# Moving the rotary exchange to SBUF-to-SBUF DMAs, and its addition, a gate polynomial and two splits to GpSimd and ScalarE, in a software-pipelined attention and expert block

## The reference

```
q, k, v = silu(causal_conv4(x @ Wq)), silu(causal_conv4(x @ Wk)), silu(causal_conv4(x @ Wv))
q, k = rope(q, cos, sin), rope(k, cos, sin)      # pairs (x1, x2) -> (x1 c - x2 s, x1 s + x2 c)
q, k = q / |q|, k / |k|
beta  = sigmoid(x @ bw + bb)
alpha = exp(-exp(A_log) * softplus(x @ gkw + gkb + dt_bias))
S     = alpha * (S - beta * k (k S)) + beta * k v      # per token, o = q S + D (q.k) v
y     = ((x @ Wg) * silu(o * rsqrt(mean(o*o)) * onorm_w)) @ Wo
```

## Time and profile before

| what | value |
|---|---|
| profiled execution, time | 5533.59 us |
| its span, first to last instruction | 5531.7 us |
| median of three runs | 5533.1 us |
| mean granted TensorE clock | 0.843 of 2.4 GHz |
| TensorE, VectorE busy | 87%, 84% of the span |
| ScalarE, GpSimd busy | 62%, 38% of the span |
| mean DMA | 36 GB/s |

### The profile page before, as it was taken

How to read it: one execution, slowest core, us unless ns; L and a number is a source line. 1 busy time by engine, 2 the same in 40 slices (tenths; PEclk the granted TensorE clock), 3 DMA queues, 4 the chain that set the end, 5 groups by cost and what they waited for, 6 DMA issues and landing times.

```text
span 5531.7 us, 111231 instructions
## 1 busy us (share of the span) xinstructions
PE 4792.2 (87%) x40448; PEld 3609.5 (65%) x40448; DVE 4623.1 (84%) x11457; ACT 3445.0 (62%) x6166; POOL 2085.5 (38%) x1485
## 2 busy tenths in 40 slices
PE   4688889988889898889898899888899888899986
PEld 2466667666667666667666677666677666677665
DVE  6888898888888888988888988888988888988852
ACT  3456666656666656766666666566666666666653
POOL 3443333443343442343443344433434433334420
PEclk7778898888888888988888888878988888888878
DMA  1001111011111011111111111111111011111011
GB/s 59 10 11 34 43 43 34 28 32 37 43 43 34 24 32 41 43 33 32 33 33 42 43 33 32 32 34 43 43 34 32 32 34 43 43 34 32 31 34 56
DMA packets 214453, 197.13 MB, mean 36 GB/s; under 512 B 13848, under 2 KB 176416, under 8 KB 209696
## 3 DMA queue, kind: packets, MB, share of 16 engines
q1 hardware_dynamic: 213920, 190.01, 11.1%
HBM read 148.02 MB, written 4.19 MB: 28 GB/s over the span
## 4 chain that ended last, share of the span: by engine, by line
DVE 52%; PE 38%; issue 8%; ACT 1%; SPq 0%; DMA 0%; POOL 0%; DVEq 0%; POOLq 0%; ACTq 0%
PE bank L984 36%; DVE acc L1390 10%; DVE tmpb L1556 6%; DVE NP L1526 6%; DVE Gam L1559 5%; DVE mx L1653 3%; DVE Gam L1512 3%; DVE moe L1738 2%; PE bank L988 2%; DVE QK L1671 1%; DVE QK L1479 1%; DVE Gam L1563 1%; DVE rot L1475 1%; DVE ms L1603 1%; DVE Kt L1543 1%
## 5 line engine op out<-in xcount | busy, mean ns | idle before, releaser
L1390 DVE SCALAR_TENSOR_TENSOR acc<-bank,conv_w,acc 128x255 f32<-128x255 f32 (+2 forms) x2304 | 925.1, 470 | 27.3 <-ACT acc L791 26.4
L717 POOL TENSOR_TENSOR sq<-acc 128x256 f32<-128x256 f32 x256 | 191.2, 747 | 1734.5 <-ACT acc L797 1722.3
L984 PE MATMUL bank<-QK 64*128 64x256 f32 (+1 forms) x4096 | 603.3, 352 | 211.8 <-DVE mx L1653 97.7
L984 PE MATMUL bank<-W,h 128*128 128x128 f32 x4096 | 579.7, 302 | 190.1 <-issue 103.3
L984 PEld LDWEIGHTS bank<-W,h 128*128 128x128 f32 x4096 | 551.7, 215 | 237.1 <-issue 129.6
L984 PE MATMUL bank<-mT,W 128*128 128x256 f32 x2048 | 626.4, 447 | 60.3 <-issue 39.7
L984 PEld LDWEIGHTS bank<-QK 64*128 64x128 f32 (+1 forms) x4096 | 288.6, 142 | 523.7 <-issue 346.0
L966 ACT ACTIVATE h<-bank,b 128x256 f32<-128x256 f32 x1024 | 416.7, 479 | 288.6 <-PE bank L984 286.7
L984 PEld LDWEIGHTS bank<-mT,W 128*128 128x128 f32 x2048 | 420.9, 220 | 219.2 <-issue 155.3
L729 POOL TENSOR_TENSOR rot<-rot,sin 128x512 f32<-128x512 f32 x256 | 337.3, 1317 | 450.8 <-DVE rot L1475 450.8
L1559 DVE TENSOR_TENSOR Gam<-Gam,tmpb 128x31 f32<-128x31 f32 (+15 forms) x992 | 448.1, 452 | 34.1
(11 more groups left out here) (226 smaller groups left out, 10275.4 us busy)
## 6 DMA issues: line engine op xcount, KB each, us to landing
W<-in_W SPq DMA_DIRECT2D x512, 256.0 KB, 3.2
QK<-QK SPq DMA_DIRECT2D x32, 1024.0 KB, 5.1
xin<-in_x SPq DMA_DIRECT2D x32, 128.0 KB, 4.7
x<-in_x SPq DMA_DIRECT2D x32, 128.0 KB, 2.1
xnG<-xnT SPq DMA_DIRECT2D x32, 128.0 KB, 1.9
out<-moe SPq DMA_DIRECT2D x32, 128.0 KB, 1.9
NP<-in_c_alpha_sel SPq DMA_DIRECT2D x1, 1024.0 KB, 5.4
Wqkv<-in_Wq SPq DMA_DIRECT2D x1, 512.0 KB, 6.1
```

Source lines behind the costliest of these rows:

```text
L984: return mm(out_, lhsT, rhs, start=first, stop=last)
L1390: v.scalar_tensor_tensor(acc[:, n % 2, m, j:T], ps[:, m, 0:T - j], conv_w[:, kind, c, PAD - j:KT - j], acc[:, n % 2, m, j:T], ALU.mult, AL ...
```

## The change

It has five parts and a new set of tables.

1. **Exchange**: `swap` leaves VectorE. SP issues two DMAs for each chunk, `acc` odd partitions to `rot` even ones and the reverse.
2. **Addition**: `rope` leaves VectorE for GpSimd, behind the sin product.
[...]
4. **Splits**: `maxes` goes to GpSimd (6 operations). Of `fqk` the two casts go to ScalarE (`part`), the last difference to GpSimd (`part2`), one difference stays. Of `alphaT` four copies go to ScalarE (`al`), three operations stay.
5. **Constants**: the scale 1/64 of the mean square goes into ScalarE's Square, so two small VectorE operations (L1609) go; the factor 2 goes into `neg_A`.

`ORDER` and `BANK` are replaced as a whole; they still span 35 turns. The load of `xnG` waits for four `g` and four `v` products of the sequence before instead of one `g`.

```diff
 ORDER = {
     "sp": """
-        xnG:0@1 x1:0@3 expert:1@3 expert:0@3 expert:2@3 expert:3@3 expert:4@3 expert:5@3 QK1:0@1 store:0@3 expert:7@3
-        expert:6@3 xin:0@0""",
+        swap:5@1 swap:6@1 xnG:0@1 expert:1@3 x1:0@3 swap:7@1 expert:0@3 expert:2@3 expert:3@3 swap:0@0 expert:4@3
+        QK1:0@1 swap:1@0 expert:5@3 swap:2@0 expert:6@3 store:0@3 swap:3@0 expert:7@3 xin:0@0 swap:4@0""",
...
@@ sync
+            def swapped(k, n):
+                sp.wait_ge(a_silu.sem, a_silu.at(k, n + 1))
+                if begun(k, n - 1):
+                    sp.wait_ge(p_QK.sem, p_QK.at(k, n - 1))
+                for q in range(2):
+                    sp.dma_start(rot[q::2, n % 2], acc[1 - q::2, n % 2]).then_inc(rot_in[n % 2][q].sem, 16)
@@ gpsimd
             def by_sin(k, c):
-                pool.wait_ge(v_rot.sem, v_rot.at(k, c + 1))
+                for q in range(2):
+                    pool.wait_ge(rot_in[c % 2][q].sem, rot_in[c % 2][q].at(k, 16 * (c // 2 + 1)))
...
+            def turned(k, c):
+                pool.wait_ge(p_rope.sem, p_rope.at(k, 2 * c + 2))
+                g.tensor_tensor(chunk(c), chunk(c), by_token(rot[:, c % 2]), ALU.add).then_inc(p_QK.sem, 1)
+            def gate(i, n):
+                pool.wait_ge(v_gate.sem, v_gate.at(i, 8))
+                g.tensor_tensor(lp2[:], lp[:], lp[:], ALU.mult).then_inc(p_gate.sem, 1)
+                g.tensor_scalar(lpp[:], lp2[:], 1.0 / 15, 1.0 / 13, ALU.mult, ALU.add).then_inc(p_gate.sem, 1)
+                for m, d in enumerate((11, 9, 7, 5, 3, 1)):
+                    g.tensor_tensor(lpp[:], lpp[:], lp2[:], ALU.mult).then_inc(p_gate.sem, 1)
+                    g.tensor_scalar(lpp[:], lpp[:], 1.0 / d, None, ALU.add).then_inc(p_gate.sem, 1)
...
+            def max_parts(j, n):
+                pool.wait_ge(v_mx.sem, v_mx.at(j, FH))
+                g.tensor_scalar(mrest[:], mx[:], -1.0, None, ALU.mult).then_inc(p_mp.sem, 1)
+                g.tensor_copy(mpart[:, 0], mrest[:]).then_inc(p_mp.sem, 1)
...
@@ scalar, first tap of chunk n
-                    act.wait_ge(v_rot.sem, v_rot.at(i, n - 1))
+                    for q in range(2):
+                        act.wait_ge(rot_in[n % 2][q].sem, rot_in[n % 2][q].at(i, 16 * (n // 2)))
@@ vector
-            def swapped(k, n):
-                v.stream_shuffle(rot[:, n % 2], acc[:, n % 2], swap).then_inc(v_rot.sem, 1)
-            def turned(k, n):
-                v.tensor_tensor(chunk(n), chunk(n), by_token(rot[:, n % 2]), ALU.add).then_inc(v_QK.sem, 1)
```

More of the change, by code:

```diff
@@ new lines @@
+        sin:4@1 cos:5@1 rope:4@1 QSadd:0@2 dots:5@1 rstd:0@0 root:0@2 QSadd:1@2 dots:6@1 norm:0@2 sin:5@1 cos:6@1
+        dots:7@1 rope:5@1 root:1@2 norm:1@2 sin:6@1 cos:7@1 rope:6@1 frstd:0@2 sin:7@1 rope:7@1 frstd:1@2 X:0@1
+        part2:0@2 cos:0@0 sin:0@0 cos:1@0 maxes:0@2 sin:1@0 dots:0@0 nrm:0@1 poly:0@0 dots:1@0 rope:0@0 rope:1@0
+        vscale:0@1 cos:2@0 vscale:1@1 sin:2@0 dots:2@0 cos:3@0 Dv:0@1 dots:3@0 sin:3@0 rope:2@0 cos:4@0 frstd:2@2
+        dots:4@0 R1:0@1 rope:3@0 R1:1@1 xs:0@2 Dv:1@1""",
@@ L111 @@
[L111 to L113 removed]
+    GT:0=1 KS:0=5 KS:1=2 QS:0=1 QS:1=7 S:0=2 Wo:0=2 alpha:0=7 alpha:1=0 alpha:2=5 alpha:3=0 alpha:4=6 alpha:5=7
+    alpha:6=5 alpha:7=6 alpha:8=3 alpha:9=4 alpha:10=1 alpha:11=7 alpha:12=1 alpha:13=6 alpha:14=5 alpha:15=1
+    alphaT:0=7 b2:0=7 cross:0=0 cross:1=1 cross:2=5 cross:3=3 ctx:0=5 ctx:1=1 ctxT:0=1 fWo:0=6 fqk:0=2 fv:0=5 g:0=3
@@ L435, in program @@
         a_siluV = signal("a_siluV", 4)
-        v_rot = signal("v_rot", NC)
+        rot_in = [[Signal(sem(f"rot_in_{m}_{q}"), 8 * NC) for q in range(2)] for m in range(2)]
         p_sq = signal("p_sq", NC)
@@ L734, in _ @@
                 "root": root, "norm": normalise, "frstd": root_ln, "xs": two_x, "vscale": scale_values, "dots": dots,
-                "cos": by_cos, "sin": by_sin})
+                "cos": by_cos, "sin": by_sin, "rope": turned, "poly": gate, "part2": last_part,
+                "maxes": max_parts})
         @block.scalar
@@ L920, in turned_h, with alpha_parts, parts @@
                     .then_inc(a_hT.sem, 1)
+            def alpha_parts(i, n):
+                if n == 0:
+                    act.wait_ge(*full_at(i, "alphaT"))
+                    if prev(i) is not None:
+                        act.wait_ge(*full_at(prev(i), "alpha", H - 1))
+                        act.wait_ge(v_alpha.sem, v_alpha.at(prev(i), 1))
+                    a_t = bank("alphaT")[0:H, 0:T].rearrange("p (t k) -> p t k", t=NT)
+                    s.copy(al1[:], a_t).then_inc(a_al.sem, 1)
+                    s.copy(alpha3[0:H, :, 2:GW], a_t[:, :, 1:P]).then_inc(a_al.sem, 1)
+                else:
+                    act.wait_ge(v_alpha.sem, v_alpha.at(i, 1))
+                    s.copy(al2[:], alr[:]).then_inc(a_al.sem, 1)
+                    s.copy(alpha3[32:32 + H, :, 2:GW], alr[:, :, 1:P]).then_inc(a_al.sem, 1)
+            def parts(j, n):
+                if n == 0:
+                    act.wait_ge(*full_at(j, "fqk"))
+                    s.copy(part[:, 0], pair(bank("fqk"))).then_inc(a_part.sem, 1)
+                else:
+                    act.wait_ge(v_part.sem, v_part.at(j, 1))
+                    s.copy(part[:, 1], prest[:]).then_inc(a_part.sem, 1)
             def repeated(j, n):
```

273 lines of the change are left out of this document (126 added, 147 removed).

## The result

The change is slower: 5689.9 us median (5657.6 to 5710.4, 4 runs) against 5536.5 us for the kernel before on the same chip, a ratio of 1.027 (95% interval 1.021 to 1.033). The forecast was 5195 us and 0.09 for slower. The page of the profiled execution (5710.39 us, span 5708.6): busy time by engine, the chain that ended last, and the two groups of solve steps.

The account below looks back on a forecast made before the run. DVE was taken to bound 126 us of each 166.9 us turn; shedding 18.7 + 3 us would leave PE leading, about 155 us a turn. Over 29 turns, 5533.6 - 348 + 10 gave about 5195 us, range 5060 to 5420.

Parts of the forecast that it names:

- DVE time is worth its length there: In the DVE-led 126 us of a turn, DVE time removed shortens the turn equally, until PE's 106.47 us take over.
- the part which DVE leads: 126 us of a 166 us turn, DVE 95% busy and PE 84%; the rotation, splits and polynomial were placed there.
- the 18.7 counted: Sum of work leaving DVE in one turn, 18.7 us: exchanges, additions, scalings, polynomial and splits; 13% of DVE's 144.1.
- PE takes over at 106.5, 95% full: In the DVE-led part, PE's 106.5 us becomes the limit; at 95% busy that is 112 us, 114 with late semaphores.
- ScalarE gets six copies ... hidden: Copies moved to ScalarE add about 2.7 us a turn, 108 to 111, hidden by its 50 us of idle time.
- 2.1 us longer for each chunk, hidden: Exchange by DMA takes 2.8 us instead of 0.73, hidden as long as the two slots of acc and rot cover it.
- the sign that the prediction had set: If right, ScalarE's taps wait for `rot<-acc` no more than 1 us a turn in total.
- 29 x 17 = 493 feared at most: If the slots fail to cover the longer exchange, eight chunks cost up to 17 us a turn, all of the gain.
- Some 2 us for late semaphores: Allowance for the longer rotation, raising the DVE-led part of a turn from 112 to 114 us.
- Rival (d): Exchanges behind expert loads on SP's queue go out late, stopping taps and DVE: 179 us a turn, 5895 us; chance 0.09.
- where I took 3: Solve steps lose 6.1 us a turn to GpSimd contention; half, 3 us, was expected back.
- rival (c): GpSimd's power `nrm` blocks DVE's solve step for 5.41 us each turn: 160.4 us a turn, 5355 us; chance 0.07.

Follow-up runs that it names:

- k1: Kernel before, with only exchanges 3 to 7 and additions 1 to 5, beside the joins, cut to a few columns: 5512.5 us, ratio 0.997.
- g1: Kernel before in its own order, all sixteen VectorE exchange and addition steps of the rotation cut to a few columns: 5450.4 us, ratio 0.986.
- e7: All moves of the change in the order and banks of the kernel before, exchange by DMA on SyncE's queue: 5615.3 us, ratio 1.016.
- f2: f3 with the addition also on GpSimd; equally e7 with the splits of alpha and feature parts back on VectorE: 5492.4 us, ratio 0.993.
- h1: The change in its own tables, with the splits of alpha and feature parts back on VectorE: 5870.4 us, ratio 1.060.
- f1: e4 with the splits of alpha and feature parts back on VectorE; polynomial, maxima and mean-square scalings stay moved: 5424.3 us, ratio 0.981.
- e4: Kernel before in its own order with only the small moves (polynomial, maxima, splits, mean square); exchange and addition stay on VectorE: 5567.7 us, ratio 1.006.
- f3: f1 with the exchange by DMA on SyncE's queue, addition still on VectorE: 5487.0 us, ratio 0.992.
- e2: The change with the exchange's DMAs issued from ScalarE's queue behind each silu instead of SyncE's: 6089.9 us, ratio 1.101.
- e9: The change with its exchange back on VectorE as a stream shuffle, set into the new order by hand: 6103.0 us, ratio 1.104.
- k2: Kernel before, with only the other six rotation steps (exchanges 0 to 2, additions 0, 6 and 7) cut to a few columns: 5449.8 us, ratio 0.985.
- e10: Kernel before in every operation, but in the order and banks of the change's tables, missing VectorE steps set in: 6800.8 us, ratio 1.231.
- e6: All moves of the change in the order and banks of the kernel before, exchange by DMA on ScalarE's queue: 5709.8 us, ratio 1.033.

## Why the prediction was wrong

Point by point, by its own steps.

- **"DVE time is worth its length there" failed, and with it the sum.** The step before it, that the rotation stands in the part which DVE leads, was wrong for ten of its sixteen steps: the table of before issues exchanges 3 to 7 and additions 1 to 5 behind `close:0@1`, beside joins in which PE is busy all of the time. Those are 7.4 of the 11.8 us of the rotation and of the 18.7 counted, and k1 measured 18 us for two thirds of their time (160 us). All sixteen gave 81 us for 254 (g1), a third of their length where the prediction took all of it, and the other six bought no shorter solve or scans either. The cut of the earlier trace rows showed that PE-led stretch with DVE busy 25.72 us in it; I did not ask whose microseconds these were.
- **"PE takes over at 106.5, 95% full": missed.** PE's idle time rose to 23.5 us instead of falling to about 7. The solve lost 18.4 us, but 21.7 came back in scans and joins. The prediction held everything outside DVE's part fixed at 40 us, but a new order can hand that filling work to other phases. This was no rival of mine; e7 against the change prices it at 75 us. Between f2 and h1, both without hops, it is 378 us, with steps set in by hand in both.
- **"ScalarE gets six copies ... hidden" failed.** ScalarE had the time but not at the moment: in the order before, the two hops, with `part2` on GpSimd, cost 143 us (f1 to e4) and 123 (f2 to e7). In the change VectorE waits 9.9 us for them and TensorE 57.6. I priced an engine's load where a place in its order was asked for.
- **"2.1 us longer for each chunk, hidden": right in the change**, where tap and sin product wait 8.0 us in all for it, by the sign that the prediction had set (1 us a turn). In the order before it costs 63 us (f1 to f3), of 29 x 17 = 493 feared at most. The landing was as forecast: 2.0 us for `rot<-acc`. "Some 2 us for late semaphores" was no term of the loss: DVE does wait 10.3 us a turn for ScalarE's first tap in the change, but ScalarE's idle time before that tap is TensorE's product (94.0 of 105.5 us), not the exchange.
- **Rival (d)** had the right sign, but not its mechanism: exchanges that go out late and stop the first tap are not in the rows of the change. What is left of SyncE's queue is the wait for expert weights, 87.9 us against 19.3 before. That "slower" came true is luck for (d).
- **Right:** DVE 126.2 us a turn (122 forecast), GpSimd 80.7 (84), PE 148.4 (148); the 24 small GpSimd steps, 0.21 to 0.33 us each (0.3); the solve steps (364.6 + 355.9) / 32 = 22.5 us a turn instead of 27.3, so contention gave 4.8 us where I took 3. Outside the solve, where I took 0, some came: `Gam<-V,Gam`, once a turn, has a median of 2.96 us instead of 1.24 (rows below).
- **No block by the power step**, rival (c), fell as forecast. GpSimd's timeline of the change has it beside the solve, and DVE's solve steps in its midst keep their 0.41 us:

```profile
2881.59 5.44 POOL L670 TENSOR_TENSOR nrm<-sk,half_c 128x32 f32<-128x32 f32 x1
```

```profile
2883.34 0.41 DVE L1607 TENSOR_TENSOR tmpb<-Gam 128x247 f32<-128x247 f32 x1
2883.78 0.42 DVE L1610 TENSOR_TENSOR Gam<-Gam,tmpb 128x247 f32<-128x247 f32 x1
...
2885.80 0.39 DVE L1607 TENSOR_TENSOR tmpb<-Gam 128x231 f32<-128x231 f32 x1
```

  The Trainium skill, SBUF — State Buffer, section "SBUF: two separate sides", has the other engine blocked for the whole instruction; the trace does not agree for this one, with at most 0.42 us for solve steps that lay wholly within its 5.44.

**What stays open:** why the new order is slower than the old one with the same placement (75 us) was seen in the phases and not undone by an experiment. The wait for expert weights is an untested candidate: 87.9 us in the change and 92.2 in e2, but 25.4 in e7 and 25.2 in e9, the new order without any exchange by DMA. Open too is what sets the granted clock of the joins. Between 0.64 and 0.74 lie 6 us of a turn, 29 x 6.2 = 180 us if all turns differed so: as much as the whole result.

## What to carry to other kernels

Price a step by the phase in which it stands, and name for each the engine that leads there: work beside a fully busy engine is nearly free, and moving it gains little (k1: 18 us for 160). A step handed to another engine is worth its time only when the result is ready before its consumer's turn comes; in the order before, where it stood close behind, each hop cost VectorE 3.6 to 3.7 us of waiting a turn (e4). Move the one and space the other together, or leave it. Before a new order is trusted, run the new placement in the old order and the other way round: here the best kernel, f1 at 5424 us, was three of the moves (polynomial, maxima, scalings) in the order before. Steps set into a finished order by hand bring losses of their own, so the comparison bounds and does not settle.

## What the runs showed of the hardware

- In joins where PE never idles, one program in one execution took 46.5 to 52.7 us a turn, as the granted clock was 0.74 to 0.64. A mean of 0.64 is TensorE at 1.2 GHz instead of 2.4 for 72% of the stretch (2 x 0.36). In the stretch after, the scans, PE has gaps (38.60 of 43.70 us) and the clock is 0.96. Over the whole span the clock was 0.84 to 0.85 in before, the change, f1 and g1 alike, so there low time mostly moved between phases, and it costs where PE leads. Not in all kernels: k2's profiled execution had 0.853, e2 and e9 0.80, e10 0.76.
- A product with two SBUF operands on VectorE and a wide one on GpSimd stretched each other. In the change DVE's `Gam<-V,Gam` takes 2.96 us, where its median was 1.24 before, beside GpSimd's two wide products. The first takes 2.34, as it does before (2.36); the second takes 2.25, where its median is 1.27:

```profile
2802.10 2.96 DVE L1663 TENSOR_TENSOR Gam<-V,Gam 128x1024 f32<-128x1024 f32 x1
```

```profile
2801.64 2.34 POOL L708 TENSOR_TENSOR Kt<-Kt,onorm 128x1024 f32<-128x1024 f32 x1
2803.94 2.25 POOL L743 TENSOR_TENSOR rot<-rot,sin 128x512 f32<-128x512 f32 x1
```

  The ends fit a wait of one for the other: GpSimd's first product ends at 2803.98, VectorE's at 2805.06, 1.08 later, and GpSimd's second at 2806.19, 1.13 after that.

- The same exchange issued by ScalarE instead of SyncE cost 400 us in the new order (e2 against the change) and 94 in the old one (e6 against e7), with the kernel before within 10 us in all of these batches.
